# Perceiver layer on one core: attention's probability transposes and weighted values as pairs of 64-row tiles into two PSUM banks each

## What is computed

```
x = x + cross_attention(layernorm(x), ctx)      # 16 heads of 32, 1601 keys, masked softmax
x = x + self_attention(layernorm(x))            # linear, one weight matrix
x = x + mixture_of_experts(layernorm(x))        # 8 experts, top 2, hidden width 2048
```

```
q, k, v = heads(x @ q_w.T + q_b), heads(ctx @ k_w.T + k_b), heads(ctx @ v_w.T + v_b)
scores = where(mask, -inf, q @ k.T / sqrt(32))      # per batch and head: 64 x 1601
out = softmax(scores) @ v
```

## Time and profile before

| what | value |
|---|---|
| median of three runs | 1251.3 us |
| profiled execution, first to last instruction | 1248.0 us |
| PE busy | 1226.0 us, 98%, 8533 products |
| DVE busy | 844.3 us, 68% |
| ACT busy | 676.0 us, 54% |
| POOL busy | 147.5 us, 12% |
| mean granted TensorE clock | 0.999 of full speed |

### The profile page before, as it was taken

How to read it: one execution, slowest core, us unless ns; L and a number is a source line. 1 busy time by engine, 2 the same in 40 slices (tenths; PEclk the granted TensorE clock), 3 DMA queues, 4 the chain that set the end, 5 groups by cost and what they waited for, 6 DMA issues and landing times.

```text
span 1248.0 us, 22257 instructions
## 1 busy us (share of the span) xinstructions
PE 1226.0 (98%) x8533; PEld 1150.7 (92%) x8533; DVE 844.3 (68%) x2213; ACT 676.0 (54%) x1202; POOL 147.5 (12%) x84
## 2 busy tenths in 40 slices
PE   7999999999999999999999999999999999999998
PEld 7899999999999999999999999999978889989996
DVE  6566656566665656666565666677689888877887
ACT  6455545645554564555456355435555666767673
POOL 0003101300310150031013003100012000000012
PEclk9999999999999999999999999999999999999999
DMA  8102200220220022022002202200326777777663
GB/s 297 38 1 91 82 2 1 99 73 1 91 82 1 1 97 76 1 91 81 2 1 99 74 1 91 96 2 1 109 71 240 259 235 269 235 245 259 228 220 129
DMA packets 61046, 126.97 MB, mean 102 GB/s; under 512 B 3644, under 2 KB 21192, under 8 KB 60824
## 3 DMA queue, kind: packets, MB, share of 16 engines
q1 hardware_dynamic: 58776, 118.97, 27.8%
q0 software_dynamic: 2176, 6.72, 1.6%
HBM read 120.01 MB, written 14.32 MB: 108 GB/s over the span
## 4 chain that ended last, share of the span: by engine, by line
PE 88%; DVE 7%; ACT 2%; issue 1%; DMA 1%; SPq 0%; ACTq 0%; DVEq 0%
PE ptp L877 25%; PE work L877 21%; PE pv L1033 7%; PE ptp L1017 7%; PE work L915 7%; PE work L1248 6%; PE work L1250 3%; PE ptp L1271 2%; PE ptp L1274 2%; PE ptp L1272 2%; PE ptp L1273 2%; PE ptp L1275 2%; DVE w_lo L1618 1%; PE work L884 1%; DVE w_lo L1624 1%; DVE pt L1530 1%
## 5 line engine op out<-in xcount | busy, mean ns | idle before, releaser
L877 PE MATMUL ptp<-vw_hi,cx_hi 128*128 128x256 f32 x832 | 241.8, 291 | 0.0
L877 PE MATMUL ptp<-vw_lo,cx_hi 128*128 128x256 f32 x832 | 235.4, 283 | 0.0
L877 PE MATMUL ptp<-vw_hi,cx_lo 128*128 128x256 f32 x832 | 235.3, 283 | 0.0
L540 POOL TENSOR_TENSOR cx_lo<-raw,cx_hi 128x1664 fp32r<-128x1664 f32 x28 | 106.3, 3795 | 669.9 <-ACT cx_hi L601 669.9
L877 PE MATMUL work<-cx_hi,kw_hi 128*128 128x400 f32 (+1 forms) x504 | 175.1, 347 | 0.8 <-DVE cx_lo L1432 0.7
L877 PEld LDWEIGHTS ptp<-vw_hi,cx_hi 128*128 128x128 f32 x832 | 159.2, 191 | 17.0 <-issue 17.0
L877 PE MATMUL work<-cx_hi,kw_lo 128*128 128x400 f32 (+1 forms) x504 | 173.7, 345 | 0.0
L877 PE MATMUL work<-cx_lo,kw_hi 128*128 128x400 f32 (+1 forms) x504 | 173.2, 344 | 0.0
L1530 DVE TENSOR_TENSOR pt<-ptp,pt 128x512 fp32r<-128x512 f32 (+1 forms) x224 | 141.0, 649 | 33.8 <-ACT pt L601 30.3
L877 PEld LDWEIGHTS ptp<-vw_hi,cx_lo 128*128 128x128 f32 x832 | 159.3, 191 | 0.0
L877 PEld LDWEIGHTS ptp<-vw_lo,cx_hi 128*128 128x128 f32 x832 | 159.2, 191 | 0.0
(11 more groups left out here) (291 smaller groups left out, 2371.8 us busy)
## 6 DMA issues: line engine op xcount, KB each, us to landing
w1raw<-in_w SPq DMA_DIRECT2D x32, 1024.0 KB, 5.0
w2raw<-in_w SPq DMA_DIRECT2D x32, 1024.0 KB, 6.2
raw<-in_ctxT SPq DMA_DIRECT2D x31, 832.0 KB, 6.2
pr<-in_mask SPq DMA_DIRECT2D x8, 800.5 KB, 4.3
xrow<-x_rows SPq DMA_DIRECT2D x7, 256.0 KB, 6.1
y_rows<-y_out_rows POOLq DMA_DIRECT2D x7, 256.0 KB, 2.6
xs<-in_x SPq DMA_DIRECT2D x1, 1024.0 KB, 9.2
qwraw<-in_qwT SPq DMA_DIRECT2D x1, 1024.0 KB, 7.8
```

The source lines that it names most:

```text
L540: pool.tensor_tensor(cx[1][:, :, sl], raw[:, k % 2], cx[0][:, :, sl].bitcast(F32), ALU.subtract).then_inc(c_lo, 1)
L877: last = pe.matmul(dst, lhs(i, c), rhs(j, c), start=(c == 0 and (i, j) == (0, 0)), stop=(c == n - 1 and (i, j) == (1, 0)))
```

## The change

Every transpose of a 128 by 128 block of pr becomes two transposes of 64 rows: rows 0 to 63 write one bank and rows 64 to 127 another. Every weighted value product of 128 rows becomes two of 64 rows, again into two banks. The eight banks are grouped into four pairs: work0/work1, work2/work3, ptp0/ptp1 and ptp2/pv. Blocks of transposes go round the pairs by the table `PAIR_OF`; both sums of a group lie in ptp2 and pv. ACT and DVE read a block across both banks of its pair in one instruction, as many elements as before.

The sums of a group now lie in two banks, so `fold` makes four copies and `group_out` four adds, and one more add of the two halves of `folded`, ahead of the four that write qT. The last group has no bank of its own any more.

In the order, t moves from behind k4 to behind s3; k5 comes ahead of w0; in the last half t comes behind s3 too, and w0 ahead of the early query. Within w0 and w1 two blocks of transposes come first, and each later one follows a product by the table `NEXT_TURN`. The banks of the other items are given by `ring_banks`.

```diff
-        steps += e[2:3] + v[6:] + e[3:]
+        steps += t + e[2:3] + v[6:] + e[3:]
...
-            steps += k[:5]
-        steps += t + k[5:6] + w[:1] + k[6:] + w[1:]
+            steps += k[:6]
+        steps += w[:1] + k[6:] + w[1:]
...
+TURNED_BY = [2, TPH + 2, 2 * TPH]
+FIRST_TURNS = [(2, 3), (TPH + 2, TPH + 3)]
+NEXT_TURN = {0: 4, 2: 5, 3: 6, 4: 7, 5: 8, 8: 11, 9: 12, 10: 13}
+PAIR_OF = [3, 3, 2, 0, 1, 2, 0, 1, 2, 1, 2, 0, 1, 2]
...
+        pairs = [top.enter_context(nc.psum_tensor(n, [P, 2, BANK], F32)) for n in ("work01", "work23", "ptp01", "ptp2_pv")]
+        sums = [ptp[2], pv]
...
+            def fold(b, g):
                 act.wait_ge(pt_used, NPT * b + TPH * (g + 1) + PTD)
+                act.wait_ge(att_rows, 4 * b + g)
+                for rows, others, cols in sum_parts():
+                    act.activation(folded[rows, 0], sums[0][rows, cols], ACT.Copy)
+                    ins = act.activation(folded[rows, 1], sums[0][others, cols], ACT.Copy)
+                ins.then_inc(folded_done, 1)
...
             def turn(b, last, j):
...
+                if jj == 0:
+                    pe.wait_ge(w_free, count(b, last, ("v", h, 5)))
+                    pe.wait_ge(pv_free, 4 * b + 2 * h + 1)
+                if jj == 2:
+                    pe.wait_ge(w_free, count(b, last, ("v", h, TPH - 1)))
+                if jj in (3, 4):
+                    pe.wait_ge(w_free, before_pair(b, last, pair, ("w", 2 * h, 0)))
+                elif jj == 11:
+                    pe.wait_ge(w_free, before_pair(b, last, pair, ("w", 2 * h + 1, 0)))
+                elif jj > 4:
+                    owner = max(i for i in range(jj) if PAIR_OF[i] == pair)
+                    pe.wait_ge(pt_lo, NPT * b + 2 * TPH * h + owner + 1 + PTD)
...
+                    for a in range(2):
+                        rows = slice(S * a, S * (a + 1))
+                        ins = pe.transpose(block[:, a, u], pr[rows, (2 * g + rt) % 4, (first + n) * P:(first + n + 1) * P],
+                                           ident[rows, rows])
...
+                        for a in range(2):
+                            rows = slice(S * a, S * (a + 1))
+                            ins = pe.matmul(sums[a][:, rt * 2 * P:(rt + 1) * 2 * P],
+                                            vv[rows, kt, g % 2, rt].rearrange("p a d -> p (a d)"),
+                                            pt[rows, j % PTD, n, rt].rearrange("p a d -> p (a d)"),
...
             def weighted(b, last, g):
+                base = 2 * TPH * (g // 2)
+                for jj in FIRST_TURNS[g % 2]:
+                    turn(b, last, base + jj)
+                for jj in range(TPH * (g % 2), TPH * (g % 2 + 1)):
+                    weigh(b, base + jj)
+                    if jj in NEXT_TURN:
+                        turn(b, last, base + NEXT_TURN[jj])
...
+            def group_out(b, g):
+                dve.wait_ge(folded_done, 4 * b + g + 1)
+                for rows, others, cols in sum_parts():
+                    dve.tensor_tensor(folded[rows, 0], sums[1][rows, cols], folded[rows, 0], ALU.add)
+                    ins = dve.tensor_tensor(folded[rows, 1], sums[1][others, cols], folded[rows, 1], ALU.add)
                 ins.then_inc(pv_free, 1)
                 dve.wait_ge(pv_free, 4 * b + g + 2)
+                dve.tensor_tensor(summed, folded[:, 0], folded[:, 1], ALU.add).then_inc(sums_done, 1)
```

More of the change, by code:

```diff
@@ L165, in by_pair, with ring_banks, before_pair @@
     return [bank[:, 0:n * 2 * P].rearrange("p (n g r d) -> p n g r d", n=n, g=2, r=2)[:, :, :, rt, :] for rt in range(2)]
+def ring_banks(last):
+    banks, scored, others, late = [], 0, 0, False
+    for kind, a, j in STEPS[last]:
+        if kind == "s":
+            banks.append(scored % 4)
+            scored, others, late = scored + 1, 0, False
+        elif kind == "w":
+            others, late = 0, True
+        elif kind in "kanq":
+            plain = others % 4 if others < 4 or last else 2 + others % 2
+            banks.append(2 if last and (kind, j) == ("k", 5) else plain)
+            others += 1
+    return banks
+BANKS = [ring_banks(False), ring_banks(True)]
 def bank_of(last, step):
-    return step[2] % PTD if spare(step) else RING[last].index(step) % 4
+    return step[2] % PTD if spare(step) else BANKS[last][RING[last].index(step)]
 def before_bank(b, last, step):
     q = RING[last].index(step)
[L176 to L180, removed]
+    bank = BANKS[last][q]
+    mine = [m for m in range(q) if BANKS[last][m] == bank]
+    if mine:
+        return count(b, last, RING[last][mine[-1]])
+    other = max(m for m in range(len(RING[0])) if BANKS[0][m] == bank)
+    return NW * b + FIRST_K + max(ITEMS[0].index(RING[0][other]) + 1 - NW, bank - 3)
+def before_pair(b, last, pair, weighed):
+    earlier = STEPS[last][:STEPS[last].index(weighed)]
+    return count(b, last, [m for m in earlier if m in RING[last] and bank_of(last, m) // 2 == pair][-1])
 def pt_before(j):
@@ L377, in layer, with sum_parts, turned_block, pt_part @@
         turn_banks = [work[1], work[2], yb[2], work[3]]
-        def sum_bank(last, g):
-            return work[3] if last and g == 3 else pv
+        def sum_parts():
+            halves = [slice(2 * HD * rt, 2 * HD * (rt + 1)) for rt in range(2)]
+            return [(halves[rt], halves[1 - rt], slice(rt * 2 * P, (rt + 1) * 2 * P)) for rt in range(2)]
+        def turned_block(j, units):
+            jj = j % (2 * TPH)
+            start = 2 * P if jj == 1 else 0
+            return pairs[PAIR_OF[jj]][:, :, start:start + units * S].rearrange("p a (u q) -> p a u q", q=S)
+        def pt_part(j, n, part):
+            return pt[:, j % PTD, 0:n, :, part, :].rearrange("p n r (a q) -> p a (n r) q", a=2)
         def scattered(ph, e):
@@ L1013, in turn @@
                 if j % TPH == 0:
                     pe.wait_ge(exp_done, 8 * b + 2 * g + 2)
-                for n in range(min(2, KT - first)):
-                    for rt in range(2):
-                        ins = pe.transpose(ptp[j % PTD][:, (2 * n + rt) * P:(2 * n + rt + 1) * P],
-                                            pr[:, (2 * g + rt) % 4, (first + n) * P:(first + n + 1) * P], ident[:])
+                units = min(4, 2 * (KT - first))
+                block = turned_block(j, units)
@@ L1024, in weigh @@
                 pe.wait_ge(pt_lo, NPT * b + j + 1 + PTD)
-                sums = sum_bank(last, g)
-                if first == 0 and sums is pv:
+                if j % (2 * TPH) == 0:
+                    pe.wait_ge(pt_lo, NPT * b + j + 2 + PTD)
+                if first == 0:
                     pe.wait_ge(pv_free, 4 * b + g + 1)
-                elif first == 0:
-                    pe.wait_ge(w_free, count(b, last, ITEMS[last][-1]))
                 for n in range(min(2, KT - first)):
@@ L1554, in body @@
                         pt_item(b, i)
[L1555 to L1559 removed]
+                    if kind == "w":
+                        group_out(b, a)
                     if last and step == ("v", 0, 1):
```

81 lines of the change are left out of this document (28 added, 53 removed).

## The result

The changed kernel takes 1257.6 us (median of four runs, 1255.9 to 1259.1) beside 1250.7 for the kernel before (four runs, 1249.9 to 1251.8; three of them gave the 1251.3 ahead of the prediction): ratio 1.0056, 95% interval 1.0042 to 1.0070. It is slower by 0.6%. The forecast was 1256 with a range of 1238 to 1271, "slower" with 0.56; as a difference of spans it was 5.3 us, and 7.3 were measured. The profiled execution's span grew from 1248.0 to 1255.3 us, at a granted clock of 0.999 before and 0.997 after.

The account below looks back on a forecast made before the run. PE's issue pace was taken to bound attention. Per half batch +0.11 -0.37 +0.10 +0.38 = +0.22 us, sixteen times 3.5, plus tail 1.8, took the span from 1248.0 to 1253.3; carried to the median, 1256 us, range 1238 to 1271.

Parts of the forecast that it names:

- What a pair costs: Pace of 64-row pairs on PE: 0.064 us a transposed pair, 0.12 us a weighted-value pair.
- second rival: A transposed pair keeps 0.11 us, as weight loads cost by columns alone: 1271 us; chance 0.14.
- third rival: Pairs don't overlap at these lengths (0.124 and 0.24 us): 1336 us; chance 0.04.
- (a): Switches between full and 64-row form: w0, now between key products, adds one in and one out, +0.38 us.
- (b): Stage t, moved behind scores s3, waits for VectorE's split of value item 5: +0.11 us a half batch.
- (c): Handover in w0 from transposes through ScalarE and VectorE to product, 1.8 us a buffer, walked: w0 5.63 us, -0.37.
- (e): w1 walked with the handovers and the longer sums: 5.67 us, +0.10 on the old 5.57.
- (d): Two sum banks behind w0 need more copies and adds; second key item free at +6.4 us, so transpose 11 waits.
- (f): After the last w1, two more copies, two adds and the wide add delay the output rows' turning: +1.8 us.
- first rival: Handovers bind less than walked; PE runs w0 and w1 at its own pace (5.1, 4.5 us): 1229 us; chance 0.34.

Follow-up runs that it names:

- turned early: Changed kernel with each later block of transposes in w0 and w1 issued one product earlier: 1262.5 us.
- one sum: Changed kernel reading only the second bank of the sums, leaving the other half of the keys out of the result: 1247.4 us.
- deferred sums: Changed kernel with both sum banks read by one whole ScalarE copy and one whole VectorE addition, the remaining additions behind the next item: 1254.8 us.
- Row weights late: Changed kernel with the last row weights moved from ahead of the early query's copy to behind the last differences of w1: 1256.1 us.
- full tiles: Changed kernel's order, bank pairs and look-ahead, but transposes and weighted values as full 128-row products with one sum bank: 1261.9 us.
- t late: Changed kernel with stage t behind value item 6 instead of behind scores s3, in the last half too: 1257.9 us.
- one query ahead: Changed kernel with the third early query product issued before the wait for the last attention rows, not behind the row turning: 1255.5 us.

## Why the prediction came out

**What a pair costs.** Right: 0.063 and 0.118 us against 0.064 and 0.12. Second and third rival fall. The Trainium skill ("TensorE: Matmul & The Clock Gate", section "LDWEIGHTS (loading the stationary operand)") has a weight load of 128 columns at some 107 ns whatever the rows. The trace agrees that the rows hardly matter to one load, though it records more time for it: 138 ns for a 64-row load of the transposes and 140 for a full one, 187 and 189 for the weighted products. But two 64-row loads start within one step of 0.063 us, so the 0.11 a pair that the second rival drew from it doesn't come, and the measurement decides. What sets the 0.063 isn't shown: a transpose of 64 rows also streams half the columns (64 for 128).

**(a) Array switches.** Right in place and near in size, if they are counted as the forecast counted them, up to the second product behind the change. Out of w0:
```profile
414.24 0.48 PE L1094 MATMUL ptp_pv<-pt,vv 64*128 64x256 f32 x4
414.65 0.45 PE L921 MATMUL work<-cx_hi,kw_hi 128*128 128x402 f32 x1
414.94 0.35 PE L921 MATMUL work<-cx_lo,kw_hi 128*128 128x402 f32 x1
```
The second key product starts 0.49 us behind the last weighted value (at 414.24+0.48-0.28 = 414.44), where it was 0.30 in the kernel before: 0.19, as forecast. On the way in, the first transpose starts 0.28 us behind the last key product where it was 0.18, and the second 0.11 behind it where the pace is 0.06: 0.14 for 0.19. Around w1 the switch changed sides: 0.14 more on the way in and 0.20 less on the way out.

**(b) t's place.** Right: +0.10 for +0.11, and it was the value split: with t behind v6 the stage falls to 0.70.

**(c) and (e), the walks.** Right together, each 0.15 off and in opposite directions. Without the gaps at its ends w0 takes 5.78 us where I had 5.63 (the table's 5.94, less 0.28 of way in, plus the last product's 0.12), and w1 424.76-419.24 = 5.52 for 5.67. T11, W9 and W12 start 1.70, 2.30 and 4.70 us into w1 where the walk had 1.80, 2.52 and 4.99. The kernel that turned early fits a buffer's turnaround as the limit: an earlier transpose brought no product sooner, because the three buffers of pt stand behind it.

**(d) The sums.** The mechanism was right (k7's split queued behind them, T11 waiting), its price was split wrongly. A half inside a batch came out 0.04 shorter where I had it 0.22 longer, though one sum shows the second bank costing 0.26 there; at a batch's start, which I had priced at nothing, it costs 0.7 a half (54.97 to 54.27).

**(f) The tail.** +1.9 for +1.8: right.

The direction and the mechanism of the handovers came out; three steps failed, in the forecast's words:
- "with its first two score reads done 0.4 us before PE wants these banks, at a batch's end too, where the mask adds 1.0 us". At a batch's start PE waits: the last of the wait rows above has seven of them, and by starts the second pair of s1 is delayed each time (the rows at 268.39). These halves cost 0.44 us more than the others: 7 times, 3 us. One sum and deferred sums take it away.
- "The last half has other work between w0 and w1 (an early query) and I price it like the rest". In it T11 waits for the copy of that query, which stands behind the sums and the row weights: 1.76 us. Row weights late takes 1.0 of it away, one sum nearly all.
- "(f) The tail" was summed up as if PE ran at one speed. The longer wait for the last rows, 2.1 us where it was 0.4, was followed by the stretch at a granted clock of 0.58 and 0.57, which cost 1.7 us more behind the row turning. The sum has nothing for it. That such a wait always brings it isn't so: the waits of 2.12 us (turned early) and 2.19 us (late row weights) at the same place didn't.

So an overcharge of 1.3 us in the halves met 1.9 and 1.7 us of losses that were missing, and inside the halves themselves 3 us at the batches' starts met a charge of 4 us too much (0.26 in each of 15). That the total came within 2 us is in part luck. The first rival, that handovers bind less, didn't come to pass: w0 and w1 take 5.78 and 5.52 us where it had 5.1 and 4.5. What could be lifted was VectorE's queue ahead of key item 7's split, and with it lifted the same pairs end at 1246.2 to 1248.7.

## What to carry to other kernels

Splitting a matrix product into two concurrent tiles can pay on PE (13 to 14 us here beside full tiles in the same order; 2.5 to 5 us are left beside the kernel before, since the order and the banks that the pairs need cost 8 to 11) and doubles what other engines do to put its results together: count these instructions on the engine that releases PE's banks, and look at which releases stand behind them in its queue. Work with no deadline goes into that engine's idle time ahead of the next release, and the bank is released first and the sum finished later. Price the last stage and the seams (a batch's start, the end) by their own rows; here they carried more of the loss than the fifteen equal halves.

## What wasn't expected of the hardware

- Two 64-row transposes into two banks go at 0.063 us a pair, four pairs in 0.41 us, and the weighted products at 0.118 us a pair of 256 columns, as fast as one product of full height (0.12).
- The wait on PE ahead of a fall of the granted clock, and the waits without one, overlap in length. In the profiled executions, waits of 2.12 us (changed kernel, ahead of 0.58 and 0.57), 1.85 and 1.77 us (t late, 0.54 and 0.50) and 2.48 us (full tiles, near its end, 0.50) were followed by a stretch at the lower level. Waits of 1.43 (deferred sums), 1.77 and 1.74 (one query ahead), 1.76 (changed kernel), 1.98 (t late), 2.19 (late row weights), 2.24 and 2.12 (turned early) and 2.73 us (one sum) were not. So the length of the wait alone doesn't decide it; what else does stays open. At the lower level sixteen products of the early queries took 6.58 us for 5.33.
- One ScalarE copy of 128x512 from a bank takes 0.59 us and four of 64x256 for the same elements 1.5 (0.38 each); on VectorE one addition of 128x512 takes 0.69 and four of 64x256 1.7 (0.42 to 0.43 each, and the one of 128x256 takes 0.43 too). Fewer partitions in an instruction saved nothing here.
